# The numerator matmuls of a linear attention, written half by half in place of alternating between the halves

## What is computed

```
x = x + attn_a(layernorm(x))   # delta rule with short convolutions, 16 heads of 8
x = x + ffn(layernorm(x))      # 8 experts, top 2
x = x + attn_b(layernorm(x))   # linear attention, 16 heads of 8
x = x + ffn(layernorm(x))
```

```
A   = einsum('bhid,bhjd->bhij', q, k) * mask
num = einsum('bhij,bhjd->bhid', A, v) + einsum('bhid,bhde->bhie', q, S)
den = sum(A, -1) + einsum('bhid,bhd->bhi', q, z) + EPS
out = num / den
S, z = S + k^T v, z + sum(k)
```

## Time and profile before

| | us |
|---|---|
| three runs | 770.42, 770.36, 780.55 |
| median | 770.42 |
| the profiled execution, its own time | 770.42 |
| its span in the profile | 768.7 |
| PE busy in the span | 629.4 (82%) |
| DVE busy in the span | 591.5 (77%) |
| ACT, POOL busy in the span | 480.5, 480.9 |

### The profile page before, as it was taken

One profiled execution on the slowest core, in us unless ns is written; L12 is line 12 of the kernel. 1 busy time (PEld: TensorE's weight loads), 2 busy tenths in 40 slices (PEclk: granted clock), 3 DMA queues, 4 the chain that ended last, 5 costly groups with the idle time before them and its releaser, 6 DMA issues.

```text
span 768.7 us, 17059 instructions
## 1 busy us (share of the span) xinstructions
PE 629.4 (82%) x5202; PEld 516.6 (67%) x5202; DVE 591.5 (77%) x1684; ACT 480.5 (63%) x1270; POOL 480.9 (63%) x550
## 2 busy tenths in 40 slices
PE   4835275897998979968787989989999899969797
PEld 3514153686776867747676667868778787959786
DVE  4497989799899999998986968768877847745235
ACT  3973748799798987946475655648275455544442
POOL 2027999699798999989748407207516724382554
PEclk9956676899999999999898999999999989979999
DMA  6231130402305022040010334335454455555652
GB/s 224 72 89 39 30 97 14 127 15 57 99 1 140 14 71 70 0 127 14 31 39 1 125 110 139 117 113 164 124 151 117 145 148 152 150 172 148 167 157 79
DMA packets 106766, 73.99 MB, mean 96 GB/s; under 512 B 44992, under 2 KB 94656, under 8 KB 106432
## 3 DMA queue, kind: packets, MB, share of 16 engines
q1 hardware_dynamic: 102080, 63.58, 28.8%
q0 software_dynamic: 4608, 9.45, 4.3%
HBM read 45.47 MB, written 27.53 MB: 95 GB/s over the span
## 4 chain that ended last, share of the span: by engine, by line
PE 22%; DVE 8%; SPq 8%; ACT 5%; issue 4%; DMA 3%; POOL 1%; DVEq 0%; ACTq 0%; POOLq 0%
PE bank L2123 3%; PE bank L2102 2%; SPq L625 2%; PE bank L2004 2%; PE bank L2053 2%; SPq L628 2%; PE bank L2151 2%; ACT prod_mem L1309 1%; DVE hist_mem L2982 1%; PE bank L2035 1%; PE bank L1866 1%; SPq L611 1%; SPq L614 1%; PE bank L1838 1%; DMA s_ys<-q_p 1%
## 5 line engine op out<-in xcount | busy, mean ns | idle before, releaser
L1838 PE MATMUL bank<-w,hid 128*128 128x128 f32 x768 | 103.1, 292 | 24.9 <-DVE y_even L2722 12.3
L1838 PEld LDWEIGHTS bank<-w,hid 128*128 128x128 f32 x768 | 98.4, 206 | 34.8 <-issue 12.7
L886 POOL TENSOR_TENSOR oq_mem<-hist_mem,q_t 128x384 f32<-128x384 f32 (+1 forms) x96 | 101.5, 1100 | 0.0
L1177 ACT ACTIVATE hid<-bank 128x512 f32<-128x512 f32 x112 | 62.5, 594 | 33.6 <-PE bank L1818 33.0
L2123 PE MATMUL bank<-w,wv 128*128 x448 | 62.1, 282 | 5.8 <-ACT q_p L1356 3.5
L1747 PE MATMUL bank<-xnT_h,wtap_h 128*128 128x512 f32 x104 | 49.4, 475 | 19.3 <-DVE qkv L2544 10.1
L2590 DVE TENSOR_REDUCE hist_mem<-hist_mem 128x64 f32<-128x320 f32 x128 | 62.3, 487 | 3.4
L2123 PEld LDWEIGHTS bank<-w,wv 128*128 128x128 f32 x448 | 55.6, 194 | 10.7 <-issue 10.5
L2580 DVE TENSOR_REDUCE u<-prod_mem 128x32 f32<-128x288 f32 x128 | 57.7, 450 | 3.4
L954 POOL DMA_INDIRECT s_xs<-xf,row_at x40 | 39.8, 994 | 32.5 <-DMA s_ys<-q_p 14.8
L1816 PE MATMUL bank<-xT_h,w_h 128*128 128x512 f32 x112 | 50.9, 454 | 9.1 <-ACT hid L1177 8.6
(11 more groups left out here) (303 smaller groups left out, 1846.0 us busy)
## 6 DMA issues: line engine op xcount, KB each, us to landing
hid<-in_w SPq DMA_DIRECT2D x72, 128.0 KB
s_qkv<-qkv SPq DMA_DIRECT2D x24, 256.0 KB, 3.4
pin<-s_xs SPq DMA_DIRECT2D x76, 64.0 KB
pin<-s_qkv SPq DMA_DIRECT2D x16, 256.0 KB, 2.8
kk<-in_w SPq DMA_DIRECT2D x30, 128.0 KB
s_ys<-q_p SPq DMA_DIRECT2D x28, 128.0 KB
s_ys<-q_t SPq DMA_DIRECT2D x28, 128.0 KB
s_xs<-zeros SPq DMA_DIRECT2D x40, 64.0 KB
```

Source lines behind the costliest of these rows:

```text
L886: tt(oq[:, :, j, :, 0:HD], s_at, bc(turned[:, n, j], 2, HD), ALU.mult).then_inc(o_part, 1)
L1177: nc.scalar.activation(hid[:, e % 2, f], bank[:, ZB + f, :], ACT.Relu).then_inc(hid_ready, 1)
L1838: last = nc.tensor.matmul(bank[:, y_bank(e, wide), tokens], hid[:, e % 2, f, tokens], w2[:, e, f], start=(f == 0), stop=(f == FC - 1))
```

## The change

Only the order of the matmuls in `lin_numer` is changed. Before, the loop over the pairs of heads n is outside and the batch p inside: each matmul is followed by one that uses the other 64 columns of the array, and the two state matmuls stand together at the end. Now the batch is outside: all eight matmuls of batch 0 and its state matmul come first, then the eight of batch 1 and its state matmul. The matmuls themselves, their operands, the waits at the head of the function and the one semaphore at its end are the same.

```diff
-                o = [bank[64 * p:64 * p + 64, numer_bank(c, j), 0:H * HV] for p in range(2)]
-                for n in range(NP):
-                    for p in range(2):
-                        last = nc.tensor.matmul(o[p][:, 2 * HV * n:2 * HV * n + 2 * HV], att[:, j % 2, n // 4, p, n % 4],
-                                                v_bd[:, 2 * j + p, n].rearrange("p r e -> p (r e)"), start=(n == 0),
-                                                stop=(c == 0 and n == NP - 1), skip_group_check=True)
-                if c:
-                    for p in range(2):
-                        b = 2 * j + p
-                        last = nc.tensor.matmul(o[p], phi_q[:, CH * b:CH * b + CH], state[:, b].rearrange("p h e -> p (h e)"),
-                                                start=False, stop=True, skip_group_check=True)
+                for p in range(2):
+                    b = 2 * j + p
+                    o = bank[64 * p:64 * p + 64, numer_bank(c, j), 0:H * HV]
+                    for r in range(2):
+                        for i4 in range(4):
+                            n = 4 * r + i4
+                            last = nc.tensor.matmul(o[:, 2 * HV * n:2 * HV * n + 2 * HV], att[:, j % 2, r, p, i4],
+                                             v_bd[:, b, n].rearrange("p r e -> p (r e)"), start=(n == 0),
+                                             stop=(c == 0 and n == NP - 1), skip_group_check=True)
+                    if c:
+                        last = nc.tensor.matmul(o, phi_q[:, CH * b:CH * b + CH], state[:, b].rearrange("p h e -> p (h e)"),
+                                         start=False, stop=True, skip_group_check=True)
                 last.then_inc(numer, 1)
```

## The result

The changed kernel takes 779.49 us (median of 20 runs, 772.98 to 789.27), the kernel before beside it 775.04 us (20 runs, 767.97 to 785.26). The ratio is 1.0055, with an interval of [1.003, 1.0081]: slower by some 4.3 us, within the 2% called no change. The prediction said 789 us. The direction was right and the size was not: 4.3 us in place of 19. The profiled execution took 782.75 us, 781.0 of them span.

What follows compares the result with a forecast made beforehand. The prediction took PE to bound chunks 1 to 6. Its terms, 16.6 there, 0 for chunk 0, 1 for chunk 7 and 1.5 for the clock, sum to 19.1 us on 770.4: 789 us, range 769 to 799.

Steps and rivals of the forecast that it cites:

- Rival A: In each numerator call, PE's look-ahead reaches over half a call, so loads still pair: 769 to 773 us, chance 0.20.
- The price of a call: Each numerator call with state costs PE 0.94 us more, about 0.75 in chunk 0.
- The loads without a seam: In a numerator call, 32 weight loads go one by one at 58 ns, 1.86 us for 0.95: +0.91 us.
- the seam: Between a call's two halves, two to five records overlap, saving 0.1 to 0.3 us; 0.25 chosen.
- the state matmuls: At each half's end the two state matmuls stand apart and need two further slots: +0.28 us a call.
- What is swallowed: In chunks 1 to 6, PE's waits absorb 6 us of 22.6 added, leaving 16.6; bounds 4 to 7.5.
- Chunk 0 and chunk 7: At both ends of the kernel: chunk 0 adds 0, at most 1 us; chunk 7 adds 1, at most 4.
- The clock: Numerator phases get emptier, so half of one more granted-clock fall is added: +1.5 us, bounds 0 to 9.
- Rival C: The clock falls in most chunks, 2.9 us lost in each of six numerator phases: 805 us, chance 0.05.
- Rival B: In each numerator call, PE's look-ahead reaches in between, say 8 of 16 records: 778 us, chance 0.14.
- D: A gain: the one clock fall at 612 us doesn't occur, and look-ahead spans half a call: 768 us, chance 0.03.

Runs made afterwards that it cites:

- e13: Kernel before with its numerator matmuls in runs of four per batch: ratio 0.9938 on a chip at 775.44 us.
- e3: Kernel before with its numerator matmuls in runs of two per batch: ratio 1.0004.
- e9: The kernel before itself, unchanged, run as a kernel of its own: ratio 1.0046 on a chip at 774.67 us.
- e2: Kernel before, alternating order kept, with the 16 matmuls of each numerator call issued twice: ratio 1.0121.
- e10: Kernel before, alternating order kept, with the set of 16 matmuls issued three times: median 805.48 us, ratio 1.0496.
- e15: Kernel before, alternating order kept, with the first four pairs of heads issued twice: ratio 0.9982.
- e1: The changed kernel once more, against the kernel before on another chip: ratio 1.0067.
- e4: Kernel before with the new order only in the calls for blocks 2 and 3 of each chunk: ratio 1.0013.
- e12: Kernel before with the new order only in chunks 1 to 6, on a chip at 774.67 us: ratio 1.014.
- e14: Kernel before, alternating order kept, with the first two pairs of heads issued twice: ratio 0.9969.
- the two nulls: The kernel before itself, unchanged, run as a kernel of its own on two chips: ratios 1.0046 and 0.9965.
- e11: Kernel before, alternating order kept, with the state matmuls ahead of the wait for the masked scores, on a chip at 774.67 us: ratio 1.0066.
- e5: Kernel before, alternating order kept, with the set of 16 matmuls issued three times, on a chip at 925.11 us: ratio 1.0679.
- e8: Kernel before with the new order only in chunks 1 to 6, on a chip at 925.11 us: 946.06 us, ratio 1.0224.
- e18: Kernel before, alternating order kept, with the first two pairs of heads issued twice, on a chip at 934.6 us: ratio 1.0058.
- e6: Kernel before with the new order only in blocks 0 and 1 of each chunk, on a chip at 925.11 us: ratio 1.0042.
- e17: Kernel before with its numerator matmuls in runs of four per batch, on a chip at 934.6 us: ratio 0.9985.

## Why the prediction was right in direction and wrong in size

**The mechanism: right.** PE doesn't reach over half a call. Rival A is refuted: 32 loads take 1.73 us, not 1.01. The runs give the reach as a series. One load each 58 ns, and 0.14 us for the last, make (1.73 - 0.14) / 0.058 + 1 = 28.4 slots for 32 loads with one seam between the halves: 3.6 loads overlap. For e13's three seams 1.32 us are 21.3 slots, 10.7 loads, 3.6 a seam. In e3 a run is four loads, and a seam every four covers nearly all (1.03 us). One reach of some 3.6 loads fits all three, inside the forecast's two to five records. The Trainium skill, TensorE: Matmul & The Clock Gate (the table at its head), gives TensorE a queue of 64 with a partial reorder window; here only these 3.6 loads are passed. The same page (What overlaps and what doesn't) lets LDWEIGHTS overlap only when the row group differs; these runs have 64-column loads of the same 128 rows side by side. The trace disagrees with that half of the rule, as the earlier trace rows had it.

**The price of a call: 0.78 us, not 0.94.** The loads without a seam gave 0.91 and the seam 0.21, near the forecast's 0.25. The term that was too high is the state matmuls: 0.78 - 0.91 + 0.21 = 0.08 us, not 0.28. This 0.08 is what is left over, not a reading. I had them apart in two slots of their own, but batch 0's runs beside batch 1's first matmuls (480.76 and 480.79 above), and it does start 0.95 us after the call's first record, as forecast. Over 24 calls that makes 18.7 us, not 22.6.

**What is swallowed: 8.7 us, not 6.** That is above the 7.5 us of the forecast's own bound, which counted three kinds of waits and not all of PE's 10.9 us of idle time (I had called these "nearly all" of it; they are 7.5). I discounted the waits on the ground that DVE's masked scores move along when the scores do. They hardly do: 5.8 of the 7.5 us are gone from the waits, and PE, which idled 11.4 us in e9's 200 us from 470 on (the row below), idles 3.7 after the change, 7.6 us less. The last 1.1 us of the 8.7 I can't place. e2, e10 and e15 show the same stock with another edit. The stretch of e9, with the columns of the earlier trace rows:

```profile
470.00:670.00 200.00, 188.64 (x2382) 160.08 (x2383) 152.99 (x555) 108.11 (x269) 86.20 (x87) 1.00 0.49 140
```

That leaves 10.0 us in the stretch, where the forecast had 16.6. The 10.0 rests on one profile of each kernel without a fall; e3 (197.7) supports the one before, and e1 (218.6, or 208.5 with 0.42 us taken off for each of its 23.9 us at half clock) the one after.

**Chunk 0 and chunk 7: nothing, as forecast or less.** From `lin_scores(0, 0)` to `lin_scores(1, 0)` the kernel before takes 37.0 and 35.5 us in two profiles, after the change 35.3 and 36.9. From chunk 7's projection to the end it is 105.2 and 105.9 against 107.2 and 104.5. The 1 us put in for chunk 7 isn't seen, though two profiles of one kernel differ by more than that.

**The clock: the step that failed most, and by its sign.** The forecast put in +1.5 us for more falls. To test it take for each execution its time at half clock, 2 x (1 - granted clock) x time; the profiled one after has 2 x 0.074 x 782.75 = 116 us. Over 108 executions of the kernel before on three chips near 775 us (one of 1523 us left out) the mean is 127 us (standard error 1.0), over 66 of the changed one 116 us (1.2). The two sets don't match chip for chip: 53 of the 66 are from the first comparison, in which the clock of the kernel before was taken for one execution alone. On e1's chip alone it is 119 us (2.9) against 125 (1.9), the same sign and half the size. The changed kernel spends *less* time at 1.2 GHz. A line through each set gives 0.35 (0.03) us of time for one more us at half clock before, and 0.43 (0.03) after. At the same 120 us the lines are at 772.1 and 781.6: **+9.5 us, close to the 10.0 of the stretch**, which comes from other data (8.1 on e1's chip alone). The 11 us less at half clock give back 11 x 0.39 = 4.3 us. That leaves 5.2, the difference of the means of these executions, 774.5 and 779.7; as each line goes through its means, this last step is bound to agree and tests nothing. The 5.2 lies within the interval of the ratio, 2.3 to 6.3 us.

In the 14 profiles on chips near 775 us the time before 430 us holds 89 to 102 us of half clock, whatever the kernel. What differs lies behind it, 9 to 47 us.

**The steps that failed, in the forecast's terms.** The 19.1 us lose 3.9 by the call's price, 2.7 by the waits, 1.0 by chunk 7 and 5.8 by the clock, from +1.5 to -4.3; that makes 5.7, against 4.3 measured in the first comparison. The first three are read in profiles; the last is a difference of means, and by e1's chip alone it would be about half as large. Without the clock the forecast had 17.6 us and 10.0 came.

**Why fewer falls?** I had argued that a call of twice the length makes the numerator phases emptier. It also fills PE's idle time in front of the scores. On the chips near 775 us the kernels that add PE time have smaller means at half clock (e2 113 us, e4 113, e10 107, e12 119, e13 111, e14 112, e15 117) than the two nulls (128 and 126) and e11, which adds none (134). So the new order isn't needed for it: e2, e10, e14 and e15 alternate. But the size doesn't follow the time added: e14 adds half as much as e15 and has the lower mean. On the two slow chips it goes the other way, 307 (e5), 311 (e8) and 309 us (e18) against 290 and 302 before, while e6 is at 290 and e17, at 287, lower. No profile of after, e2, e4, e10 or e15 has a fall between 454 us and chunk 7, but e1, e12, e13 and e14 have one or two and e9, a kernel before, has none. That idle time is what matters is thus argued, not shown; no run changed it alone. **Rival C** (falls in most chunks) is refuted: 0 and 1 in two profiles. **Rival B**, 778 us, is nearest to the 779.49, but only because the base has moved from 770.42 to 775.04: it had +7.6 us, A at most +2.6, and +4.3 lies between the two. Its reach of 8 records isn't there either. **D** didn't occur.

**Open:** what decides where the clock falls; why two chips need 925 and 935 us; whether runs of four are a gain.

## What to carry to other kernels

Two matmuls on different column halves of the array share a weight-load slot only while they stand close: alternate them, or keep runs to two matmuls a half; a run of eight gives all of the overlap back but some 3.6 loads at the seam. Before you count time added to the leading engine, add up its idle time in that stretch: it is a stock. Here time added to every call cost about half until it was spent and nine tenths from then on, and time added only behind the scores of a chunk (e4) cost two thirds. And where the granted clock falls now and then, make the comparison at equal time at half clock as well, since two profiles, one with and one without a fall of 24 us, differ by 10 to 11 us, more than this change is worth.

## What was not expected of the hardware

The two halves' matmuls start out of program order at the seam: five records of batch 1 start ahead of the second record of batch 0's state matmul at 480.92, and two of them ahead of its first at 480.76. The time at half clock varies between executions of one program from 114 to 140 us (the middle eight in ten of the kernel before) and carries most of the spread of its time. And chips differ: on two of them every kernel that ran there, the kernel before too, takes 920 us or more, though the first 200 us pass as on the others.
